# Cross attention key stacks filled from SBUF in narrow transfers, and projections split out of PSUM

## The chip, the cores and the metric

The kernel runs on one core of one Trainium2 chip. The metric is the time of the device for the whole program, in microseconds (us); the time before is the median of three runs. The chip has TensorE (PE in the profile; its weight loads are PEld), VectorE (DVE), ScalarE (ACT), GpSimd (POOL) and SyncE (SP), which here only issues transfers.

## What is computed

Four layers run over 32 sequences of 100 tokens with 128 features (`T` = 3,200 tokens, a chunk is four sequences, 400 tokens). Layers 0, 1 and 3 are transformer layers, layer 2 is a router layer that the change doesn't touch. A transformer layer has self attention, cross attention to a context of 1,444 tokens a sequence, and an MLP. The cross attention of layer 0 is this (16 heads of 8 features):

```
q_c = _ln(x) @ W_qc + b_qc
kv_c = _ln(context) @ W_kvc + b_kvc
k_c, v_c = split(kv_c, 2)
w = softmax(einsum('bhqd,bhsd->bhqs', q_c, k_c) * scale)
x = x + (einsum('bhqs,bhsd->bhqd', w, v_c) merged) @ W_cproj + b_cproj
```

Layer 1 takes the context without a norm, and layer 3 takes it turned, as layer 1 has kept it in memory.

## The kernel before

The phases follow one another, with a barrier between two. Every product of queries and keys is made from three bfloat16 parts of each float32 number (high, middle, low), whose six products of parts stand below one another as rows of a *stack*: the contraction over the stack's rows gives the score in nearly full precision.

**Projections** (`project_phase`, line 379). TensorE projects eight chunks into the eight banks of PSUM. VectorE copies a chunk with bias and scale to the float32 buffer `sq` (line 438). ScalarE makes the high part (170), GpSimd subtracts it from `sq` (180), ScalarE makes the middle part (173), GpSimd the low one (184); each step runs over all eight chunks before the next begins. With two projections (queries and keys of self attention) the second read of a chunk waits for the first low part of it, as `sq` is shared. SP stores a chunk when its low part is there (191; for the cross attention queries, 200, two transfers a chunk).

**Cross attention** (`cross_attention_phase`, 951) takes one sequence, or batch, a time, in a pipeline of slots written out by hand: in the slot of batch b TensorE makes the scores and values of b, the maximum tiles of b + 1 (from tile 16) and, from the last third of the slot, those of b + 2; it turns and projects the context of b + 3, and SP loads that of b + 5. Three buffers (`LAG`) exist of the stacks, values and contexts, but one of the parts `kparts` and one of the float32 keys `kf`. The work of a slot on each queue:

- TensorE: twelve blocks of context tokens; in each two groups of scores (1124), four maximum tiles (1103), the values (1141) and some of the preparation (1072, 1080, 1086). The scores of a batch wait for its negated maxima in the query stack.
- VectorE: 48 row maxima from PSUM (1260), then the row maximum, its negation and its three parts (1266 to 1284).
- ScalarE: the exponentials (1215) and copies of the preparation (1181, 1187, 1193).
- GpSimd: `pool_split_keys` (1328), the four steps that make the parts of the keys of b + 3, in one piece (layer 0) or three. It waits until the parts of the batch before have been written to memory. In layer 0 it also norms the context.
- SP (`sp_slot`, 1415), in this order: `sp_stacks` (1365) of b + 2, the load of the context, `sp_out` (1402) of b - 1, which stores the sums, waits for them, and brings them back rearranged, the store of the turned context (layer 1), `sp_negmax` (1380) of b + 1, and `sp_keys_out` (1394) of b + 3.

The key stack has 2 x 64 rows for eight pairs of heads. Before, `sp_keys_out` writes the parts in six transfers into a stack in memory (`ctx_k_stack`), whose rows of ones have been written there once, in layer 0, from a buffer that VectorE clears (1482) and SP stores (1517). `sp_stacks` waits for the scores of the batch that used the buffer and for the writes, and loads the whole stack in one transfer of all 128 partitions (1371); then it loads the queries in twelve transfers of eight partitions (1378). Self attention (line 801) loads its query stacks in twelve transfers of eight partitions from memory, and its key stacks (804) in six of 16 partitions.

## Time and profile before

| | |
|---|---|
| median of three runs | 5857.7 us (5855.48 to 5859.36) |
| the profiled execution, its own time | 5862.12 us |
| its span, first to last instruction | 5859.9 us |
| busy share of the span | PE 85%, DVE 66%, ACT 50%, POOL 26% |
| moved by transfers | 764.81 MB in 481,590 packets |
| mean granted TensorE clock | 0.897 |

The span is the time from the first to the last instruction of the profiled execution; the 2.2 us around it are the start and end of the program. The busy share is an average over phases with different limits, so the change is to be read from the phases it touches: the three cross attention phases, and the projection phases ahead of self and cross attention. A granted clock of 1.00 is 2.4 GHz, 0.50 is 1.2 GHz. In the rows of a stretch the numbers stand in the order PE, PEld, DVE, ACT, POOL (busy us and instructions), granted clock, share of the 16 DMA engines, GB/s. In rows in order of time, "idle before" is the time that the engine stood still ahead of the row, with what released it.

### The profile page before, as it was taken

How to read it: one execution, taken by the hardware profiler on the slowest of the kernel's cores; microseconds unless marked ns; L12 is line 12 of the kernel's file. 1: busy time of each engine (PE TensorE's matmuls, PEld its weight loads, DVE VectorE, ACT ScalarE, POOL GpSimd, SP SyncE). 2: the span in 40 equal slices, each digit the busy share in tenths (PEclk: the TensorE clock that was granted, in tenths of full speed). 3: DMA queues.
4: the chain of work that ended last, by engine and by line, in shares of the span. 5: the costliest groups of instructions: out<-in, count | busy, mean ns of one | idle time of the engine just before them, and what ended most of it. 6: DMA issues, size and time to landing. Idle time of an engine off the chain costs nothing. (4 is left out here: it accounts for less than half of the span.)

```text
span 5859.9 us, 149756 instructions
## 1 busy us (share of the span) xinstructions
PE 4994.4 (85%) x63358; PEld 3189.8 (54%) x63358; DVE 3843.7 (66%) x7732; ACT 2905.6 (50%) x4287; POOL 1546.6 (26%) x1270
## 2 busy tenths in 40 slices
PE   4848999999997577999999987899586899999998
PEld 2624555555563443666666653565363466666664
DVE  4537788788864445777777762544353688888883
ACT  2324666666664232666666654213223356666655
POOL 2034344344310213332333310000302333333320
PEclk6667999999997666999999998999766799999998
DMA  3334554554520525566555520530241555555540
GB/s 80 64 87 149 163 162 150 171 155 153 170 84 10 91 54 173 186 192 193 172 187 185 190 89 25 190 124 0 54 74 45 172 178 177 180 178 175 178 144 16
DMA packets 481590, 764.81 MB, mean 131 GB/s; under 512 B 144922, under 2 KB 381882, under 8 KB 468538
## 3 DMA queue, kind: packets, MB, share of 16 engines
q1 hardware_dynamic: 472090, 744.18, 42.8%
q10 hardware_dynamic: 8832, 11.07, 0.9%
q8 instruction: 500, 8.19, 0.6%
q14 instruction: 168, 1.38, 0.1%
HBM read 465.48 MB, written 287.75 MB: 129 GB/s over the span
## 5 line engine op out<-in xcount | busy, mean ns | idle before, releaser
L1260 DVE TENSOR_REDUCE maxima<-ps 100x1 f32<-100x482 f32 (+1 forms) x4608 | 2719.9, 649 | 834.3 <-PE ps L1103 827.6
L1215 ACT ACTIVATE probs<-ps 128x800 f32<-128x800 f32 (+1 forms) x2304 | 1799.4, 835 | 606.9 <-PE ps L1124 605.0
L1103 PE MATMUL ps<-kst,qst 48*100 48x482 bf16 (+1 forms) x4608 | 1102.7, 412 | 100.7 <-DMA qst<-cross_q_parts 49.5
L1312 POOL TENSOR_TENSOR kparts<-kf,zero 128x512 bf16<-128x512 f32 (+2 forms) x448 | 545.9, 1219 | 2109.1 <-ACT kf L1187 2069.8
L1141 PE MATMUL ps<-probs,vals 128*9 128x100 f32 x36864 | 1012.8, 250 | 5.5 <-ACT probs L1215 0.8
L1124 PE MATMUL ps<-qst,kst 128*128 128x200 bf16 (+1 forms) x9216 | 999.6, 251 | 11.9 <-DMA qst<-nparts 5.8
L1124 PEld LDWEIGHTS ps<-qst,kst 128*128 128x128 bf16 (+1 forms) x9216 | 761.7, 98 | 266.0 <-issue 152.5
L1141 PEld LDWEIGHTS ps<-probs,vals 128*9 128x9 f32 x36864 | 734.5, 90 | 255.4 <-issue 225.5
L1103 PEld LDWEIGHTS ps<-kst,qst 48*100 48x100 bf16 x4608 | 335.7, 120 | 617.9 <-DVE maxima L1260 326.6
L1193 ACT ACTIVATE vals<-ps 128x512 f32<-128x512 f32 (+1 forms) x288 | 161.9, 562 | 494.0 <-PE ps L1086 494.0
L1187 ACT ACTIVATE kf<-ps,perm_b_L 128x512 f32<-128x512 f32 (+1 forms) x288 | 190.4, 661 | 356.8 <-PE ps L1080 346.1
L1080 PE MATMUL ps<-ctxT,perm_wk_L 128*128 128x512 f32 (+1 forms) x576 | 306.6, 635 | 64.6 <-DVE maxima L1260 32.5
L729 ACT ACTIVATE probs<-ps 100x800 f32<-100x800 f32 x192 | 159.7, 837 | 365.3 <-PE ps L677 364.2
L1343 POOL TENSOR_TENSOR kparts<-kf,kparts 128x512 bf16<-128x512 f32 (+2 forms) x224 | 306.2, 1367 | 17.6
L1339 POOL TENSOR_TENSOR kf<-kf,kparts 128x512 f32<-128x512 f32 (+2 forms) x224 | 305.0, 1362 | 17.6
L741 DVE TENSOR_REDUCE maxima<-ps 100x4 f32<-100x400 f32 x384 | 205.2, 570 | 141.0 <-PE ps L655 140.4
L655 PE MATMUL ps<-kst 96*100 96x100 bf16 x1152 | 142.1, 285 | 146.6 <-DMA kst<-k_parts 118.1
L1086 PE MATMUL ps<-wkv_L,ctxT 128*128 128x128 f32 (+1 forms) x1536 | 227.9, 293 | 36.6 <-DVE maxima L1260 33.5
L1086 PEld LDWEIGHTS ps<-wkv_L,ctxT 128*128 128x128 f32 (+1 forms) x1536 | 184.3, 190 | 91.7 <-DVE maxima L1260 79.1
L655 PEld LDWEIGHTS ps<-kst 96*100 96x100 bf16 x1152 | 117.4, 190 | 172.0 <-issue 119.9
L180 POOL TENSOR_TENSOR sq<-sq,parts 128x400 f32<-128x400 f32 x72 | 65.7, 944 | 540.1 <-ACT parts L170 540.0
L1072 PE MATMUL ps<-ident,ctok 128*128 128x128 f32 (+1 forms) x768 | 131.6, 292 | 89.6 <-POOL ctok L1325 47.3
(253 smaller groups left out, 4634.4 us busy)
## 6 DMA issues: line engine op xcount, KB each, us to landing
kst<-ctx_k_stack SPq DMA_DIRECT2D x96, 2888.0 KB
ctx_k_stack<-kparts SPq DMA_DIRECT2D x192, 541.5 KB
ctx_k_stack<-kparts SPq DMA_DIRECT2D x192, 361.0 KB
ctok<-in_ctx_dram SPq DMA_DIRECT2D x64, 704.0 KB
ctx_k_stack<-kparts SPq DMA_DIRECT2D x192, 180.5 KB
ctx_turned<-ctxT SPq DMA_DIRECT2D x32, 722.0 KB, 3.4
cT<-ctx_turned SPq DMA_DIRECT2D x32, 722.0 KB, 5.7
ctxT<-ctx_turned SPq DMA_DIRECT2D x32, 722.0 KB
```

What stands on the lines that cost most here:

```text
L655: ins = nc.tensor.matmul(ps[0:N, o:o + N], queries[s][0:SROWS, h // 2, q0:q0 + N], keys[0:SROWS, h // 2, k0:k0 + N], start=True, stop=True)
L741: nc.vector.tensor_reduce(maxima[:, t // 4, c:c + 4], ps[0:N, at:at + CH].rearrange("p (h k) -> p h k", h=4), AX.X, ALU.max).then_inc(m_re ...
L1080: ins = nc.tensor.matmul(ps[:, at:at + w], wk, turned[s][:, a:a + w], start=True, stop=True)
L1086: ins = nc.tensor.matmul(ps[0:n, at + 128 * q:at + 128 * q + 128], turned[s][:, 128 * kt:128 * kt + n], wv, start=True, stop=True)
L1103: nc.tensor.matmul(ps[0:N, at:at + w], g.qst[s][row0:row0 + CROWS, j, N * e:N * e + N], g.kst[s][row0:row0 + CROWS, j, a:a + w], start=Tru ...
L1124: ins = nc.tensor.matmul(ps[0:kts[kt], o:o + 2 * N], g.kst[s][0:KROWS, 4 * hf + jj, 128 * kt:128 * kt + kts[kt]], g.qst[s][0:KROWS, 4 * hf ...
L1141: ins = nc.tensor.matmul(ps[q:q + VW, o:o + N], vals[s][:, kt, h, :], probs[kt % 2][hf][:, N * (2 * jj + e):N * (2 * jj + e) + N], start=( ...
L1215: nc.scalar.activation(probs[kt % 2][hf][0:kts[kt], :].rearrange("p (k n) -> p k n", k=2), src, ACT.Exp).then_inc(exp_done, 1)
L1260: nc.vector.reduce_max(maxima[:, col:col + 1], ps[0:N, at:at + widths[c]], AX.X).then_inc(m_read, 1)
L1312: return nc.gpsimd.tensor_tensor(out, src, g.zero[0:src.shape[0], 0:1].to_broadcast(list(src.shape)), ALU.add)
L1339: nc.gpsimd.tensor_tensor(kf[:, a:z], kf[:, a:z], parts[:, 0, a:z], ALU.subtract).then_inc(split, 1)
L1343: nc.gpsimd.tensor_tensor(parts[:, 2, a:z], kf[:, a:z], parts[:, 1, a:z], ALU.subtract).then_inc(parts_ready, 1)
```

## The change

*Cross attention.* There is no stack in memory any more. `sp_stacks` waits for the scores as before and for the parts of the keys, then issues twelve transfers, six rows of the stack for each of the two halves; each goes from 64 partitions of `kparts` to eight partitions of the stack, 64 rows of 2,888 bytes (1,444 bfloat16 numbers). The twelve query loads follow. `sp_keys_out` is gone. GpSimd now waits for these twelve transfers of the batch before (`k_loaded`) before it splits the next keys, and TensorE's first maximum tile waits for all twelve. The rows of ones stand in the three stacks in SBUF: in every layer VectorE clears all three stacks at the start of the phase, and SP waits for that ahead of its first slot. The six stores of ones are gone.

*Projections.* The four steps of a split are interleaved by chunk. Chunks that are `banked` keep their float32 value in the PSUM bank, and VectorE makes their two subtractions there; the others go through `sq` and GpSimd as before. With one projection (the queries of cross attention) the even chunks are banked; with two, all chunks of the second, and none of the first. The second projection no longer waits for the first to leave `sq`. The stores wait for the count of the engine that made the low part.

```diff
-def act_split(g, act, f, parts, f_ready, high, rest, middle):
-
-    for c in chunks(act):
-        act.wait_ge(f_ready, c + 1)
-        g.nc.scalar.activation(parts[:, 0, bass.ds(c * CH, CH)], tok(f, c), ACT.Copy).then_inc(high, 1)
-    for c in chunks(act):
-        act.wait_ge(rest, c + 1)
-        g.nc.scalar.activation(parts[:, 1, bass.ds(c * CH, CH)], tok(f, c), ACT.Copy).then_inc(middle, 1)
-
-
-def pool_split(g, pool, f, parts, high, rest, middle, low):
-
-    for c in chunks(pool):
-        pool.wait_ge(high, c + 1)
-        g.nc.gpsimd.tensor_tensor(tok(f, c), tok(f, c), parts[:, 0, bass.ds(c * CH, CH)],
-                                  ALU.subtract).then_inc(rest, 1)
-    for c in chunks(pool):
-        pool.wait_ge(middle, c + 1)
-        g.nc.gpsimd.tensor_tensor(parts[:, 2, bass.ds(c * CH, CH)], tok(f, c),
-                                  parts[:, 1, bass.ds(c * CH, CH)], ALU.subtract).then_inc(low, 1)
...
+class Split:
+
+
+
+    def __init__(self, sem, i, banked, parts, f):
+        self.banked, self.parts, self.f = banked, parts, f
+        self.f_ready, self.high, self.middle = sem(f"proj_read{i}"), sem(f"high{i}"), sem(f"middle{i}")
+        self.dve_rest, self.pool_rest = sem(f"dve_rest{i}"), sem(f"pool_rest{i}")
+        self.dve_low, self.pool_low = sem(f"dve_low{i}"), sem(f"pool_low{i}")
+
+    def part(self, k, c):
+        return self.parts[:, k, CH * c:CH * c + CH]
+
+    def value(self, g, c):
+        return bank(g, c) if c in self.banked else tok(self.f, c)
+
+    def nth(self, c):
+        return len([x for x in range(c + 1) if (x in self.banked) == (c in self.banked)])
+
+    def rest(self, c):
+        return self.dve_rest if c in self.banked else self.pool_rest
+
+    def low(self, c):
+        return self.dve_low if c in self.banked else self.pool_low
+def dve_split(g, dve, s, full, bias, scale):
+    for c in range(NCH + 2):
+        if c < NCH:
+            dve.wait_ge(full, c + 1)
+            g.nc.vector.tensor_scalar(s.value(g, c), bank(g, c), bias, scale, ALU.add, ALU.mult).then_inc(s.f_ready, 1)
+        if 0 <= c - 1 < NCH and c - 1 in s.banked:
+            dve.wait_ge(s.high, c)
+            g.nc.vector.tensor_tensor(bank(g, c - 1), bank(g, c - 1), s.part(0, c - 1), ALU.subtract).then_inc(s.dve_rest, 1)
+        if 0 <= c - 2 < NCH and c - 2 in s.banked:
+            dve.wait_ge(s.middle, c - 1)
+            g.nc.vector.tensor_tensor(s.part(2, c - 2), bank(g, c - 2), s.part(1, c - 2), ALU.subtract).then_inc(s.dve_low, 1)
+
+
+def act_split(g, act, s):
+    for c in range(NCH + 1):
+        if c < NCH:
+            act.wait_ge(s.f_ready, c + 1)
+            g.nc.scalar.activation(s.part(0, c), s.value(g, c), ACT.Copy).then_inc(s.high, 1)
+        if c:
+            act.wait_ge(s.rest(c - 1), s.nth(c - 1))
+            g.nc.scalar.activation(s.part(1, c - 1), s.value(g, c - 1), ACT.Copy).then_inc(s.middle, 1)
+
+
+def pool_split(g, pool, s):
+    copied = [c for c in range(NCH) if c not in s.banked]
+    for c, before in zip(copied + [None], [None] + copied):
+        if c is not None:
+            pool.wait_ge(s.high, c + 1)
+            g.nc.gpsimd.tensor_tensor(tok(s.f, c), tok(s.f, c), s.part(0, c), ALU.subtract).then_inc(s.pool_rest, 1)
+        if before is not None:
+            pool.wait_ge(s.middle, before + 1)
+            g.nc.gpsimd.tensor_tensor(s.part(2, before), tok(s.f, before), s.part(1, before), ALU.subtract).then_inc(s.pool_low, 1)
...
-        f_ready = [sem(f"proj_read{i}") for i in range(npart)]
-        high = [sem(f"high{i}") for i in range(npart)]
-        rest = [sem(f"rest{i}") for i in range(npart)]
-        middle = [sem(f"middle{i}") for i in range(npart)]
-        low = [sem(f"low{i}") for i in range(npart)]
+        banked = [(), tuple(range(NCH))] if npart == 2 else [tuple(range(0, NCH, 2))]
+        splits = [Split(sem, i, banked[i], parts[i], sq) for i in range(npart)]
...
-                    for c in chunks(dve):
-                        dve.wait_ge(full[i], c + 1)
-                        if i:
-                            dve.wait_ge(low[i - 1], c + 1)
-
-                        nc.vector.tensor_scalar(tok(sq, c), bank(g, c), bias, scale, ALU.add,
-                                                ALU.mult).then_inc(f_ready[i], 1)
+                    dve_split(g, dve, splits[i], full[i], bias, scale)
...
-    K_RUNS = ((0, 3), (3, 2), (5, 1))
-    KW = 16 * 2 * len(K_RUNS)
+    KL = 16 * 2 * len(SLOT_K)
...
-                wait(g.pe, k_loaded[s], 16 * (r + 1))
+                wait(g.pe, k_loaded[s], KL * (r + 1))
...
-            wait(pool, k_written[p.s], KW * (p.r + 1))
+            wait(pool, k_loaded[p.s], KL * (p.r + 1))
...
             wait(sp, st_full, H2 * (b - LAG + 1))
-            wait(sp, k_written[s], KW * (r + 1))
-            sp.dma_start(g.kst[s][:, :, :].rearrange("p j n -> p (j n)"), g.kscr[s]).then_inc(k_loaded[s], 16)
+            wait(sp, parts_ready, len(CUTS) * (b + 1))
+            for slot, part in enumerate(SLOT_K):
+                for e in range(2):
+                    at = HALF * e + HD * slot
+                    src = parts[HALF * e:HALF * e + HALF, part, :]
+                    sp.dma_start(g.kst[s][at:at + HD, :, :], src).then_inc(k_loaded[s], 16)
...
-        def sp_keys_out(k):
-            b, s, r = k.b, k.s, k.r
-            sp = g.sp
-            wait(sp, parts_ready, len(CUTS) * (b + 1))
-            for first, n in K_RUNS:
-                for e in range(2):
-                    sp.dma_start(slot_rows(s, e, first, n), parts[HALF * e:HALF * e + HALF, 0:n, :]).then_inc(k_written[s], 16)
...
-            if slot.k(3) is not None:
-                sp_keys_out(slot.k(3))
...
-                if normed:
-                    nc.vector.memset(g.kst[0][:, :, :].rearrange("p j n -> p (j n)").bitcast(F32), ONE_PAIR).then_inc(stacks_set, 1)
+                for s in range(LAG):
+                    nc.vector.memset(g.kst[s][:, :, :].rearrange("p j n -> p (j n)").bitcast(F32), ONE_PAIR).then_inc(stacks_set, 1)
...
-                if normed:
-                    sp.wait_ge(stacks_set, 1)
-                    for s in range(LAG):
-                        for e in range(2):
-                            rows = slice(HALF * e + CROWS, HALF * e + HALF)
-                            sp.dma_start(g.kscr[s][rows, :], g.kst[0][rows, :, :].rearrange("p j n -> p (j n)")).then_inc(ones_written, 16)
-                    sp.wait_ge(ones_written, 16 * 2 * LAG)
+                sp.wait_ge(stacks_set, LAG)
```

## Rows read from the trace of the kernel before

**Rows 1.** Busy time by engine in a stretch of each cross attention phase; then clock, DMA share, GB/s
```profile
600.00:1600.00 1000.00, 923.45 (x14169) 594.18 (x14167) 811.17 (x1987) 659.52 (x916) 422.14 (x200) 1.00 0.51 158
2400.00:3400.00 1000.00, 949.31 (x14837) 621.94 (x14836) 768.73 (x1404) 616.39 (x882) 322.57 (x312) 1.00 0.58 185
4700.00:5600.00 900.00, 850.68 (x13907) 557.33 (x13909) 735.78 (x1343) 545.19 (x771) 312.49 (x300) 1.00 0.57 177
```

**Rows 2.** Waits in 2400 to 3400 us: us in total, times, longest
```profile
PEld ps L1124 <- DMA qst<-nparts: 2.2, 4, 1.5
```

**Rows 3.** Order in time of SP's queue, one batch of layer 1: start, us, issue
```profile
2795.63 4.13 SPq L1387 DMA_DIRECT2D qst<-nparts  x6
2799.81 8.54 SPq L1400 DMA_DIRECT2D ctx_k_stack<-kparts  x6
...
2811.55 0.33 SPq L1371 DMA_DIRECT2D kst<-ctx_k_stack  x1
2811.92 8.35 SPq L1378 DMA_DIRECT2D qst<-cross_q_parts  x12
...
2826.51 2.56 SPq L1411 DMA_DIRECT2D oT<-o_sums  x4
...
2834.04 4.13 SPq L1387 DMA_DIRECT2D qst<-nparts  x6
```

**Rows 4.** Order in time of TensorE, last scores and first new maximum tile
```profile
2798.84 0.86 PE L1124 MATMUL ps<-qst,kst 128*36 128x200 bf16 x8
...
2829.76 0.42 PE L1103 MATMUL ps<-kst,qst 48*100 48x482 bf16 x2
```

**Rows 5.** Order in time of VectorE, row maxima of two batches, layers 0 and 3
```profile
1053.49 0.20 DVE L1266 TENSOR_REDUCE rowmax<-maxima 100x16 f32<-100x48 f32 x1
...
1093.84 0.20 DVE L1266 TENSOR_REDUCE rowmax<-maxima 100x16 f32<-100x48 f32 x1
...
5109.82 0.20 DVE L1266 TENSOR_REDUCE rowmax<-maxima 100x16 f32<-100x48 f32 x1
...
5146.00 0.20 DVE L1266 TENSOR_REDUCE rowmax<-maxima 100x16 f32<-100x48 f32 x1
```

**Rows 6.** Stretches with one kind of transfer each; last two columns: DMA share, GB/s
```profile
100.00:102.50 2.50, 0.00 (x0) 0.00 (x0) 0.00 (x0) 0.00 (x0) 0.09 (x1) 0.50 1.11 318
2801.10:2803.90 2.80, 2.64 (x46) 1.63 (x45) 2.33 (x5) 1.57 (x2) 0.00 (x0) 1.00 0.98 198
2804.00:2810.00 6.00, 5.76 (x76) 4.26 (x78) 4.02 (x8) 3.12 (x5) 0.00 (x0) 1.00 0.93 273
1949.00:1951.50 2.50, 0.00 (x0) 0.00 (x0) 0.00 (x0) 0.00 (x0) 0.00 (x0) 0.50 0.58 50
1950.50:1954.00 3.50, 0.00 (x0) 0.00 (x0) 0.00 (x0) 0.00 (x0) 0.00 (x0) 0.50 0.58 75
1960.00:1967.50 7.50, 6.08 (x44) 4.94 (x43) 5.77 (x12) 0.00 (x0) 0.00 (x0) 0.50 0.59 76
2244.00:2246.50 2.50, 0.00 (x0) 0.00 (x0) 0.00 (x0) 0.00 (x0) 2.41 (x3) 0.50 0.64 141
```

**Rows 7.** Order in time at the start of layer 1's phase: GpSimd, SP, TensorE
```profile
2211.41 1.04 POOL L1312 TENSOR_TENSOR kparts<-kf,zero 128x512 bf16<-128x512 f32 x1 [7.05 <-ACT kf L1187]
...
2224.57 8.57 SPq L1400 DMA_DIRECT2D ctx_k_stack<-kparts  x6
...
2247.04 1.01 PE L1103 MATMUL ps<-kst,qst 48*100 48x482 bf16 x3 [20.51 <-DMA qst<-cross_q_parts]
```

**Rows 8.** Order in time of VectorE, layer 0: the memset of a key stack
```profile
397.66 4.87 DVE L1482 MEMSET kst<- 128x5776 f32 x1 [1.15 <-issue]
```

**Rows 9.** VectorE's read of PSUM (line 438); order in time of GpSimd and SP
```profile
L438 DVE TENSOR_SCALAR sq<-ps,perm_b_L x24: 632/634/636, 363.5 to 4501.9; 128x400 f32<-128x400 f32 x24
...
373.70 10.57 SPq L200 DMA_DIRECT2D cross_q_parts<-parts  x16
...
85.67 7.23 POOL L180 TENSOR_TENSOR sq<-sq,parts 128x400 f32<-128x400 f32 x8
```

More of the change, by code:

```diff
@@ L188, in sp_parts_out @@
-def sp_parts_out(g, sp, parts, dram, low, stored):
+class Split:
[14 more added lines that the diff above has]
+        return self.dve_low if c in self.banked else self.pool_low
@@ L189, in sp_parts_out, with sp_queries_out @@
+def sp_parts_out(g, sp, parts, dram, split, stored):
     for c in chunks(sp):
-        sp.wait_ge(low, c + 1)
+        sp.wait_ge(split.low(c), split.nth(c))
         sp.dma_start(dram[:, :, bass.ds(c * CH, CH)], parts[:, :, bass.ds(c * CH, CH)]).then_inc(stored, 16)
     sp.wait_ge(stored, 16 * NCH)
-def sp_queries_out(g, sp, parts, low, stored):
+def sp_queries_out(g, sp, parts, split, stored):
     for c in range(NCH):
-        sp.wait_ge(low, c + 1)
+        sp.wait_ge(split.low(c), split.nth(c))
@@ L418, in _ @@
                     pe_linear(g, pe, [w], [lambda c: tok(xin, c)], xin_ready, xin_per, free, full[i])
-                    free = f_ready[i]
+                    free = splits[i].f_ready
             @block.vector
@@ L450, in _ @@
                 for i in range(npart):
-                    act_split(g, act, sq, parts[i], f_ready[i], high[i], rest[i], middle[i])
+                    act_split(g, act, splits[i])
             @block.gpsimd
@@ L455, in _ @@
                 for i in range(npart):
-                    pool_split(g, pool, sq, parts[i], high[i], rest[i], middle[i], low[i])
+                    pool_split(g, pool, splits[i])
             @block.sync
@@ L461, in _ @@
                     if dram is g.qx:
-                        sp_queries_out(g, sp, parts[i], low[i], stored[i])
+                        sp_queries_out(g, sp, parts[i], splits[i], stored[i])
                     else:
-                        sp_parts_out(g, sp, parts[i], dram, low[i], stored[i])
+                        sp_parts_out(g, sp, parts[i], dram, splits[i], stored[i])
 class attention_close_sems:
@@ L1013, in cross_attention_phase @@
         split, parts_ready = sem("split_steps"), sem("parts_ready")
-        k_written, k_loaded = slots("k_written"), slots("k_loaded")
+        k_loaded = slots("k_loaded")
         qst_loaded, neg_loaded = slots("qstack_loaded"), slots("negmax_loaded")
@@ L1020, in cross_attention_phase @@
         ones, zeros, ctx_std, stacks_set = sem("ones"), sem("zeros"), sem("ctx_std"), sem("stacks_set")
-        ones_written, queries_zeroed, ctx_kept = sem("ones_written"), sem("queries_zeroed"), sem("ctx_kept")
+        queries_zeroed, ctx_kept = sem("queries_zeroed"), sem("ctx_kept")
         set_up = 1 + 2 * LAG
-        def slot_rows(s, e, first, n):
-            return g.kscr[s].rearrange("(e r d) (j n) -> e (d j) r n", e=2, d=HD, j=PAIRS)[e, :, first:first + n]
         def max_tile(slot, x):
@@ L2039, in program @@
     g.ctxT = nc.dram_tensor("ctx_turned", (B, P, S), F32).ap()
-    g.kscr = [nc.dram_tensor(f"ctx_k_stack{s}", (P, PAIRS * S), BF16).ap() for s in range(LAG)]
     g.oself = [nc.dram_tensor(f"o_self_sums{s}", (P, CH), F32).ap() for s in range(LAG)]
```

## The prediction, made before the change was run

> **What bounds the kernel now.** I read the stretches first. In the three cross attention phases, which fill about 3,900 of the 5,860 us, TensorE is busy 92 to 95 per cent of the time at the full granted clock (1.00, the 2.4 GHz level), VectorE 77 to 82, and the transfers take a share of 0.51 to 0.58 of the 16 DMA engines [rows 1]. The reader is to see that TensorE has little idle time left for anyone to give back. The waits of 1,000 us of layer 1 say the same from the other side: the only transfer that TensorE waits for is that of the negated maxima, 2.2 us in four waits of weight loads [rows 2]; the key stacks are never waited for there. So in the steady part the trip through memory costs nothing, and the change can gain only at the edges; it can lose wherever the new transfers are later than the old ones.
>
> The queue of SyncE (SP) shows how much later they may be. One batch of layer 1 takes 38.41 us, from the maxima issue at 2795.63 to the next at 2834.04. In it SP spends 8.54 us on six writes of parts to memory, waits until 2811.55 for them to land, spends 0.33 us on the wide load and 8.35 us on twelve query loads; after the sums of the batch before are out it waits again, until 2826.51 [rows 3]. TensorE ends the last scores of a batch at about 2799.7 and first uses the next batch's stack at 2829.8, 30 us later [rows 4]. The other two layers run at 40.35 us and 36.18 us a batch [rows 5].
>
> **The change, part by part.**
>
> *Removed:* per batch six writes (8.54 us of SP, 2.22 MB), the wait behind them, and one load of 2.96 MB. None is on the path in the steady part.
>
> *Added:* twelve transfers of 64 rows of 2,888 bytes, 2.22 MB in all, each from 64 partitions into eight. They can be issued as soon as SP has sent the maxima and the old stack is free, near 2799.8 in the batch shown, 11.75 us ahead of today's load. Issue costs SP about 0.70 us each by the query loads of the same shape (8.35 over twelve) [rows 3], 8.4 us together. What decides is D, the time in which the data moves. The trace of before has no such transfer, so I bound it from both sides.
>
> - Upper speed: a store over all partitions moves 318 GB/s on 16 engines [rows 6]. Loads into eight partitions keep the share at 0.58, that is, they use eight engines [rows 6]. Half of 318 is 159 GB/s, and D = 2.218 MB / 159 = 14 us.
> - Lower speed: while only one half of the parts is read (64 partitions) all 16 engines are busy at 0.98 and yet move 198 GB/s; once both halves are in flight it is 273 [rows 6]. Something that belongs to the partitions saturates. By plain proportion eight would get 24.8 GB/s, which the next rows exclude; the slowest stretch in which transfers into few partitions ran in a backlog is 50 GB/s [rows 6], D = 44.4 us.
> - The nearest row: self attention loads its query stacks with transfers of just this form, 64 rows, eight engines, eight partitions of destination, and in a backlog they run at 75 and 76 GB/s, twice over [rows 6]. Its rows are shorter (800 bytes) and come from memory. I take 76: D = 29.2 us. That it is above 50 I read as neighbouring transfers overlapping on different partitions.
>
> The Trainium skill says, in SBUF — State Buffer, section "Door 1: The DMA port swizzle (why [64,N] ≈ [32,N])", that DMA bandwidth follows the number of SBUF ports that the partitions reach, and gives 196 GB/s for 64 partitions and 104 for 16. The 198 of the trace agrees with it; by that rule eight partitions would get about half of 104, an estimate of 52 GB/s and a D near 43 us. It speaks against this change, where the 76 of the trace is milder.
>
> *What D does.* Two loops close over one batch. (A) The parts have one buffer: GpSimd may not split the next keys before the last narrow transfer has landed, where it now waits only for the writes. From the first issue: 1.3 us to the first data, D, 1.5 us to landing (both as in rows 3 and 6: issue 2799.81, data from 2801.1, data until 2810, next step 2811.55), then the split, 13.1 us from 2211.41 to 2224.5 [rows 7], and 0.2 us of signals: D + 16.1. (B) SP is in order. The sums stand in the same DMA rings behind the keys, 2.5 us of queries [rows 6], about 2.3 us of the next context and 0.5 of their own, and SP waits for them; then come 3.6 us of small issues and 4.2 us for the maxima [rows 3], and only then the next keys: 1.3 + D + 2.5 + 2.3 + 0.5 + 1.5 + 3.6 + 4.2 = D + 15.9; without the context store of layer 1, D + 15.5 in layer 0. Behind SP's wait stand the maxima, and behind those TensorE's scores.
>
> With D = 29.2: layer 0, 44.7 against 40.35, +4.35; layer 1, 45.3 against 38.41, +6.9; layer 3, 45.3 against 36.18, +9.1. Together 20.3 us for each batch; 29 of the 31 intervals count, since two in the filling are longer already: +590 us.
>
> *Filling.* At the start of each phase the maxima wait for stack and queries: now 22.5 us from the last split (2224.57 to 2247.04) [rows 7]. After: 1.3 + D + 2.5 + 1.5 = 34.5 us, +12 in each of three phases: +36.
>
> *Clearing.* Three memsets of a stack (4.87 us each, 14.6) [rows 8] stand in place of one and six stores. VectorE has nothing to do before 2247, and the parts that SP waits for come at 2224.5, past 2202 + 14.6 = 2217 [rows 7]. I cost them at nothing; uncovered they would be 10 to 15 us a phase.
>
> *Projections.* The query projection of cross attention is paced by its stores: GpSimd's first low part is ready at 373.7, 10.2 us after the first read of PSUM at 363.5, and SP then needs 10.57 us for sixteen issues [rows 9]. With even chunks split by VectorE out of PSUM and steps interleaved, the first low part comes after about 4 us (0.63 per read, some 0.55 for each following step); the stores end at 14.6 at the earliest, and near 16 because odd chunks still take two GpSimd steps of 0.90 us: 4 to 6 us gained, 4.7 taken, times three is 14. The double projections are now one unbroken GpSimd row, 32 steps of 0.90 us (eight in 7.23) [rows 9]. After, GpSimd does the queries (14.5 us) and ScalarE, which is in order, starts on the keys only then; VectorE needs 8 x (0.63 + 0.57 + 0.57) = 14.2 us for them. 28.7 against 29: I take 1.3 us each, 4 together. Sum -18.
>
> **Sum.** +590 + 36 - 18 = +608 us on the profiled execution, whose span is 5859.9 and whose own time is 5862.1, 4.4 above the median of 5857.7. On the median that is 6465 us.
>
> **Rivals.**
>
> *The narrow transfers are quick enough; faster.* For it: the 76 may come from reading short rows of memory, which is not done here, and eight engines at their full pace give 159. The Trainium skill adds, in DMA: Bandwidth & Descriptors, section "Why small descriptors are slow (HBM only)", that SBUF to SBUF transfers don't suffer from small pieces; no run here shows it yet. Against it: the 198 of the trace, which is a read of SBUF itself with the same long rows. Its price: with D = 14 nothing closes, the filling is bound by issue (8.4 + 8.35 + 3.0 = 19.7 against 22.5, -2.8 three times), so 5857.7 - 18 - 8 = 5831 us. It decides where 3(D - 17.2) + 29(D - 20.1) = 18, at D = 20.4 us, that is 109 GB/s. Chance 0.36, and 0.06 for a rate so near this point that nothing can be told.
>
> *No overlap at all; much slower.* Twelve transfers at 50 GB/s, D = 44.4: 29 x (19.5 + 22.1 + 24.3) + 82 - 18 = +1,975, 7,833 us. For it: these transfers are 3.6 times as long as the ones that gave 76, so neighbours overlap less; this is also where the port rule leads. Chance 0.14.
>
> *The projections don't gain:* stores stay the pace, and 18 shrinks to 8. The quick case would then be 5841 us, still faster.
>
> **How the numbers follow.** The forecast, 60 to 109 GB/s around 76, has 0.44, its own range being 5,880 to 7,200. Slower in all: 0.58, faster 0.36, same 0.06; 0.2 per cent (12 us) is about what a measurement of this kernel can tell from no change. The range goes from 5,825, a little below the quick case, to 7,300, which is D near 38.5 us, 58 GB/s; it leaves out most of the case without overlap. TensorE's granted clock is 0.50 (1.2 GHz) in stretches where it had stood idle [rows 6]; waits long enough to bring that back would add to the slow cases, and I leave them at the upper end.
>
> **What would show it.** A share near 0.5 and about 76 GB/s at the start of every batch; GpSimd's first key step waiting for the keys' transfer and not for ScalarE; SP waiting longer for the sums; TensorE waiting for the stacks or the maxima; batches of about 45 us in all three layers. If instead the batches stay at 40.35, 38.41 and 36.18, D is under 20 us and I am wrong in its term alone. If they grow and GpSimd doesn't wait for transfers, it is loop B and not A.

## The result, and the profile after the change

The changed kernel takes 7207.4 us, median of four runs (7189.1 to 7219.1); the kernel before, timed beside it, 5856.6 us. The ratio is 1.230, 95% interval 1.228 to 1.232: 1,350.8 us slower. The forecast was 6465 us, slower too, but by 608 us.

The stretches of the three cross attention phases come first, as in [rows 1] (TensorE, its weight loads, VectorE, ScalarE and GpSimd busy, then the granted clock, the DMA share and GB/s):

```profile
600.00:1600.00 1000.00, 772.67 (x10903) 489.76 (x10901) 632.10 (x1528) 509.01 (x707) 319.72 (x152) 0.87 0.50 66
2800.00:3800.00 1000.00, 755.81 (x10868) 487.30 (x10871) 569.72 (x1029) 453.09 (x648) 238.99 (x232) 0.85 0.54 80
5600.00:6500.00 900.00, 655.11 (x9559) 418.06 (x9560) 512.75 (x923) 375.45 (x531) 214.47 (x208) 0.83 0.48 66
```

TensorE was busy 92 to 95 per cent at the full clock; now it is 73 to 77 per cent at a mean of 0.83 to 0.87. The DMA share has hardly moved, but the bytes behind it fell from 158 to 185 GB/s to 66 to 80: the same occupation of the engines carries less than half. The waits of the whole execution (microseconds, times, longest) name who stands still:

```profile
POOL kparts L1335 <- DMA kst<-kparts: 3369.2, 93, 41.9
...
PE ps L1126 <- issue: 836.9, 90, 14.7
...
PE ps L1126 <- DMA qst<-cross_q_parts: 137.2, 6, 31.9
```

GpSimd waits for the new transfers before each split, 93 times for 96 batches. TensorE waits 96 times at line 1126, the maximum tiles, 974 us in all. Ninety of these are put down to "issue", that is, to nothing the profile shows; what they really are comes out below. SP's queue in one batch of layer 1, against [rows 3] (start, duration, issue):

```profile
3071.83 9.06 SPq L1398 DMA_DIRECT2D kst<-kparts  x12
3080.94 22.48 SPq L1405 DMA_DIRECT2D qst<-cross_q_parts  x12
3103.47 2.58 SPq L1385 DMA_DIRECT2D ctok<-in_ctx_dram  x1
...
3112.30 0.36 SPq L1426 DMA_DIRECT2D o_sums<-osb  x1
3117.28 2.60 SPq L1430 DMA_DIRECT2D oT<-o_sums  x4
...
3120.97 4.48 SPq L1414 DMA_DIRECT2D qst<-nparts  x6
3125.97 9.04 SPq L1398 DMA_DIRECT2D kst<-kparts  x12
```

and GpSimd and TensorE in the same batch, each line ending with the idle time before it and what ended it:

```profile
3111.91 1.04 POOL L1335 TENSOR_TENSOR kparts<-kf,zero 128x512 bf16<-128x512 f32 x1 [40.46 <-DMA kst<-kparts]
```

```profile
3115.11 0.64 PE L1126 MATMUL ps<-kst,qst 48*100 48x482 bf16 x2 [13.17 <-issue]
```

The keys are first issued at 3071.83 and have landed at 3111.9, 40 us later; the query loads, issued behind them, took 8.35 us of SP before and now 22.48, because the issue itself is held up; TensorE gets its first new maximum tile at 3115.11, 3.2 us after the keys, where the old kernel had it 30 us after the start of the batch [rows 4]; the next keys go out at 3125.97. That batch is 54.1 us long. The stretches inside such a transfer give its rate (last three columns: clock, DMA share, GB/s):

```profile
3133.00:3136.00 3.00, 2.83 (x27) 2.61 (x26) 1.27 (x3) 1.31 (x3) 0.00 (x0) 1.00 0.53 61
3136.00:3139.00 3.00, 2.84 (x46) 1.86 (x45) 2.37 (x4) 1.45 (x3) 0.00 (x0) 1.00 0.52 60
...
3169.00:3172.00 3.00, 2.16 (x13) 1.32 (x11) 2.18 (x6) 1.03 (x2) 2.76 (x4) 0.50 0.06 13
```

The last of them lies behind TensorE's wait in the next batch: the granted clock is at 0.50, the 1.2 GHz level. The first two show the rate, 60 to 61 GB/s at a share of 0.52: 2.218 MB take 36 us, not 29. From the first to the last row maxima of a phase (31 intervals) a batch takes 52.07, 52.23 and 52.55 us in the three layers; before it took 39.99, 38.28 and 36.18. Single batches lie between 39 and 64 us. The means add up to 31 x (12.08 + 13.95 + 16.37) = 1,314 us of the 1,351. At the start of layer 0's phase the way from the first key issue to the first maximum tile is 43.2 us, where from the issue of the writes behind the last split it was 22.75:

```profile
415.49 8.95 SPq L1398 DMA_DIRECT2D kst<-kparts  x12
```

```profile
458.67 1.01 PE L1126 MATMUL ps<-kst,qst 48*100 48x482 bf16 x3 [30.58 <-DMA qst<-cross_q_parts]
```

### The profile page after: what moved, and what is told of

The parts are those of the page before. It is cut to its first block and busy times, and to the rows that moved or that the text cites. A ratio compares the mean times of both kernels' runs of the same rounds, so it can differ in the third digit from the quotient of the medians.

```text
span 7187.2 us, 150216 instructions
## 1 busy us (share of the span) xinstructions
PE 5298.2 (74%) x63358; PEld 3347.7 (47%) x63358; DVE 3950.7 (55%) x7812; ACT 2906.8 (40%) x4287; POOL 1477.3 (21%) x1198
## 5 line engine op out<-in xcount | busy, mean ns | idle before, releaser
L1126 PE MATMUL ps<-kst,qst 48*100 48x482 bf16 (+1 forms) x4608 | 1154.1, 447 | 1023.8 <-issue 836.9
L1164 PE MATMUL ps<-probs,vals 128*9 128x100 f32 x36864 | 1136.2, 268 | 96.6 <-issue 89.1
L1147 PE MATMUL ps<-qst,kst 128*128 128x200 bf16 (+1 forms) x9216 | 1101.7, 266 | 29.8 <-issue 18.5
L1164 PEld LDWEIGHTS ps<-probs,vals 128*9 128x9 f32 x36864 | 813.7, 96 | 402.4 <-issue 310.9
L1147 PEld LDWEIGHTS ps<-qst,kst 128*128 128x128 bf16 (+1 forms) x9216 | 829.5, 104 | 324.7 <-issue 220.7
L1103 PE MATMUL ps<-ctxT,perm_wk_L 128*128 128x512 f32 (+1 forms) x576 | 325.9, 670 | 57.9 <-DVE maxima L1283 30.0
L1103 PEld LDWEIGHTS ps<-ctxT,perm_wk_L 128*128 128x128 f32 x576 | 100.0, 206 | 164.5 <-DVE maxima L1283 102.9
```

The source lines that it names most:

```text
L1103: ins = nc.tensor.matmul(ps[:, at:at + w], wk, turned[s][:, a:a + w], start=True, stop=True)
L1126: nc.tensor.matmul(ps[0:N, at:at + w], g.qst[s][row0:row0 + CROWS, j, N * e:N * e + N], g.kst[s][row0:row0 + CROWS, j, a:a + w], start=Tru ...
L1147: ins = nc.tensor.matmul(ps[0:kts[kt], o:o + 2 * N], g.kst[s][0:KROWS, 4 * hf + jj, 128 * kt:128 * kt + kts[kt]], g.qst[s][0:KROWS, 4 * hf ...
L1164: ins = nc.tensor.matmul(ps[q:q + VW, o:o + N], vals[s][:, kt, h, :], probs[kt % 2][hf][:, N * (2 * jj + e):N * (2 * jj + e) + N], start=( ...
```

## The experiments

### Which part of the change costs and which gains

**Projections alone** (cross attention as before; the classes and loops of the projections as changed).

```
 cross_attention_phase: as before, with ctx_k_stack in memory
 project_phase: Split, dve_split, act_split, pool_split as in the change
```

> The projections of the change alone, cross attention as before. My terms of the prediction: 14 us for the three query projections and 4 us for the double ones, so 5839 us (-18). Rival: the stores of the parts are the pace and stay it, -8 us, 5849 us. If the batches of cross attention still take 40.35, 38.41 and 36.19 us, the projections have no part in the 1,350 us.

Measured: 5823.8 us against 5854.8, ratio 0.9947 (0.9934 to 0.9960): -31 us, batches unchanged. The gain is real and larger than worked out. SP's stores show where, against [rows 9]:

```profile
73.67 12.22 SPq L229 DMA_DIRECT2D q_parts<-parts  x8
88.08 8.26 SPq L229 DMA_DIRECT2D k_parts<-parts  x8
...
99.73 4.15 SPq L830 DMA_DIRECT2D kst<-q_parts  x12
...
366.60 12.24 SPq L238 DMA_DIRECT2D cross_q_parts<-parts  x16
```

The query projection's stores now end at 378.84, 16.1 us after the first read of PSUM at 362.79; before it was 384.27 - 363.49 = 20.8. The difference is the 4.7 us of the prediction to the tenth. The double projection, for which I had taken 1.3 us, gave more: the first stack load of self attention starts at 99.73 and started at 104.25, 4.5 us. Both were read in layer 0 alone; three times their sum is 27.6 of the 31 us.

**Keys alone** (projections as before).

```
 project_phase, act_split, pool_split: as before
 cross_attention_phase: as in the change
```

> The key stacks alone by narrow transfers (with the three memsets), projections as before. Theory: all of the loss is here, so the time of the whole change plus what the projections gain: 7207 + 18 = 7225 us. With the rival on the projections (-8) it is 7215 us. Batches of 52.1 to 52.5 us in all three layers, as in the whole change.

Measured: 7239.2 us, ratio 1.2367 (1.2348 to 1.2386), +1,384 us; batches 51.93, 52.62 and 52.56 us. The two parts add up: 1,384 - 31 = 1,353 against 1,351. Of the 1,384 the batches are 31 x (11.94 + 14.34 + 16.38) = 1,322, and the 62 left are some 21 us for each of the three fillings: from the last split to the first maximum tile it is 43.2, 44.1 and 44.1 us here, and 22.8, 22.5 and 22.6 in the kernel before. The memsets have no part in that: in the changed kernel the first keys of all three phases go out 0.03 us after the last step of the split, and the memsets have ended 7.0, 3.8 and 0.7 us before.

### What sets the rate of the transfers

**Half of the keys** (the upper 64 partitions left out).

```
-                for e in range(2):
+                for e in range(1):
```

> The transfers into the upper 64 partitions are left out, six of twelve with half of the bytes; the rest of the computation runs on what the memset left there. Theory that a rate holds (36 us for 2.2 MB, 62 GB/s): 18 us for 1.1 MB, below the 20 us at which the loops close, so the batches are back at 40.35, 38.41 and 36.2 us and the time is near 5835 us. Rival, that the time of a batch goes by something else than the length of the transfers (TensorE's stalls, the clock at 0.81): batches stay above 45 us and the time above 6400 us. If two transfers on opposite halves were really working side by side, half of them would take nearly as long as all: batches of 45 us or more too, but with the share of the DMA engines at half of what it is now.

Measured: 5933.4 us, one run; batches 40.78, 39.26 and 37.67 us. Most of them are back at the old length to the hundredth, with some of 42 to 46 us between them (the last section has what is known of them). The six transfers of the lower half run at the rate that the twelve of both had, and take half the time, 18.1 us on average from the first packet to the last against 35.8:

```profile
2822.00:2825.00 3.00, 2.92 (x50) 1.76 (x46) 3.00 (x6) 1.76 (x3) 0.00 (x0) 1.00 0.55 66
2825.00:2828.00 3.00, 2.83 (x25) 2.49 (x24) 1.43 (x3) 1.16 (x3) 0.00 (x0) 1.00 0.54 62
```

So it is a rate, and transfers into opposite halves of SBUF do not run side by side on SP's queue.

**The same bytes into 48 partitions** (16 transfers; the stacks then hold keys in another arrangement).

```
-            for slot, part in enumerate(SLOT_K):
+            for slot in range(PAIRS):
                 for e in range(2):
-                    at = HALF * e + HD * slot
-                    src = parts[HALF * e:HALF * e + HALF, part, :]
-                    sp.dma_start(g.kst[s][at:at + HD, :, :], src)...
+                    src = parts[HALF * e:HALF * e + CROWS, SLOT_K[slot % 6], :]
+                    sp.dma_start(g.kst[s][HALF * e:HALF * e + CROWS, slot, :], src)...
```

> The same bytes (2.2 MB a batch) from the same parts, but as sixteen transfers of 48 rows into 48 partitions, where it was twelve of 64 rows into 8; the stacks then hold other numbers, so the result is another. Theory that the eight partitions of the destination set the rate: it goes up to between 198 GB/s (the trace's read of 64 partitions) and 273, D is 8 to 11 us plus issue of 16 x 0.7, and the batches are back at 40.35, 38.41 and 36.2 us: 5835 us. Rival, that transfers inside SBUF are slow whatever their shape (rows of 2,888 bytes, 64 descriptors each): D stays at 30 us or more and the time above 6,900 us.

Measured: 5808.8 us, batches 40.35, 38.41 and 36.19 us. The transfers run at

```profile
2811.00:2814.00 3.00, 2.76 (x45) 1.64 (x45) 3.00 (x7) 1.57 (x2) 0.00 (x0) 1.00 0.89 227
2814.00:2817.00 3.00, 3.00 (x31) 2.61 (x35) 0.98 (x2) 1.61 (x3) 0.00 (x0) 1.00 0.79 201
```

A transfer inside SBUF with rows of 2,888 bytes is not slow as such. This run alone leaves open whether more partitions or more engines (a share of 0.79 to 0.89, not 0.52) make it fast; the runs with other row orders decide that.

**From memory instead of SBUF** (two transfers put the parts in memory; the same twelve load the stacks from there).

```
-                    src = parts[HALF * e:HALF * e + HALF, part, :]
+                    src = g.kscr[s][HALF * e:HALF * e + HALF, part, :]
```

> The parts go to memory first (two transfers), and the same twelve narrow transfers of 64 rows of 2,888 bytes then load the stacks from there. Theory that the destination's eight partitions are the bound: the rate stays at 60 to 66 GB/s though the source is memory, GpSimd waits no longer for the stacks (its loop is gone), but the queue's loop (D + 15.5) still makes batches of 51 to 52 us: 7100 to 7250 us. Rival, that the source in SBUF was slow: D falls to 14 to 20 us and the time to 5830 to 5900 us.

Measured: 7396.4 us, one run; batches 53.82, 54.97 and 53.90 us. The rate is

```profile
3105.00:3108.00 3.00, 2.84 (x33) 2.06 (x22) 1.84 (x4) 1.45 (x4) 0.00 (x0) 1.00 0.50 63
3108.00:3111.00 3.00, 2.84 (x47) 1.68 (x44) 2.33 (x4) 2.07 (x4) 0.00 (x0) 1.00 0.53 66
```

at the same share as from SBUF. The source plays little part: on average the keys take 32.4 us from the first packet to the last, against 35.8. (The batches are 2 us longer still, since SP also waits for the writes.)

**Eight partitions, but six apart** (and the query stacks to match).

```
-                    at = HALF * e + HD * slot
+                    at = HALF * e + slot
-                    sp.dma_start(g.kst[s][at:at + HD, :, :], src)...
+                    sp.dma_start(g.kst[s][at:at + 43:6, :, :], src)...
```

> The rows of the stacks in another order: row 6d + slot where it was 8 slot + d, so that each of the twelve transfers writes eight partitions that lie six apart and not side by side (the query stacks, which must match, too). The same count of transfers, rows and bytes. Theory that neighbouring partitions share a way in and that this set the 62 GB/s: the rate goes up to at least 109 GB/s and, with eight engines at their pace in the trace, to 159; D is 14 to 20 us, the batches are back at 40.35, 38.41 and 36.19 us and the time is 5800 to 5830 us. The Trainium skill, SBUF - State Buffer, section Door 1, gives 8 adjacent partitions two ports (an estimate of 52 to 54 GB/s) and these eight rows seven of them. Rival, that eight partitions or eight engines are slow wherever they lie: nothing changes, 7207 us and batches of 52 us.

Measured: 5820.0 us against 5856.4, ratio 0.9943 (0.9930 to 0.9957); batches 40.35, 38.41 and 36.18 us.

```profile
2817.00:2820.00 3.00, 2.92 (x46) 1.69 (x46) 3.00 (x6) 1.69 (x3) 0.00 (x0) 1.00 0.51 164
2820.00:2823.00 3.00, 2.83 (x27) 2.56 (x26) 1.34 (x3) 1.25 (x3) 0.00 (x0) 1.00 0.52 155
```

The same twelve transfers, rows and bytes, the same eight engines (share 0.51), and 2.6 times the rate. The 159 GB/s that the prediction worked out as the pace of eight engines is met.

**Two apart.**

```
-                    at = HALF * e + HD * slot
+                    at = HALF * e + 16 * (slot // 2) + slot % 2
-                    sp.dma_start(g.kst[s][at:at + HD, :, :], src)...
+                    sp.dma_start(g.kst[s][at:at + 15:2, :, :], src)...
```

> Between the change (the eight partitions of a transfer side by side) and the spread order (six apart): now two apart, over 16 partitions. Theory that groups of neighbouring partitions share a way in, so that the rate goes by how many groups are reached: twice as many as side by side, 62 x 2 = 124 GB/s, D near 18 us, just under the 20 us where the loops close: batches at 40.35, 38.41 and 36.19 us with some longer ones, 5820 to 5930 us. Rival, that it is the eight partitions together with something that only the wide spacing avoids: 62 GB/s and 7200 us.

Measured: 5834.4 us, ratio 0.9966 (0.9954 to 0.9978).

```profile
2823.00:2826.00 3.00, 2.92 (x69) 1.86 (x57) 3.00 (x6) 2.15 (x3) 0.00 (x0) 1.00 0.51 117
2826.00:2829.00 3.00, 2.84 (x23) 2.38 (x23) 1.80 (x4) 0.79 (x2) 0.00 (x0) 1.00 0.52 117
```

Twice the span of partitions, twice the rate (60 to 117), at the same share of the engines and still with eight partitions a transfer. With the six-apart order at 155 to 164, still at that share, the rate rises with how far the written partitions spread; 48 partitions at 201 to 227 use more engines. By the Trainium skill, SBUF — State Buffer, section "Door 1: The DMA port swizzle (why [64,N] ≈ [32,N])", groups of four neighbours share a port: eight side by side reach two of 16, two apart four, 48 partitions eight, an estimate of 54, 109 and 218 GB/s. The traces agree, with 60, 117 and 201 to 227; the first two lie 7 to 11 per cent above the estimates. Six apart, the eight rows reach six or seven ports by that mapping, an estimate of 163 to 190 GB/s, so there the pace of eight engines, 159, comes first.

### Which loop turns 36 us of transfer into 52 us of batch

**GpSimd's loop (A) opened:** the parts are freed one by one.

```
-            wait(pool, k_loaded[p.s], KL * (p.r + 1))      (ahead of the whole split)
+            wait(pool, k_in[0][p.s], ...)  ahead of the copies of part 0
+            wait(pool, k_in[1][p.s], ...)  ahead of part 1
+            wait(pool, k_in[2][p.s], ...)  ahead of part 2
```

> GpSimd waits for the parts one by one: the transfers go in the order of the parts, the first part may be overwritten after six of twelve, and only the last three steps of the split wait for the last transfer. Loop A shrinks from D + 16.1 to about D + 6.2 us; loop B (SP's queue in order, D + 15.5 to 15.9) is as it was. Theory that both loops were closed at almost the same length: batches of 51 to 52 us still, 7150 to 7207 us. Rival, that GpSimd's loop alone was the bound: batches of 43 to 47 us and a time of 6200 to 6800 us.

Measured: 7196.9 us, ratio 1.2290 (1.2273 to 1.2306); batches 51.99, 52.41 and 52.22 us. The numbers are those of the theory of two equal loops, but a third loop gives them too, as the next runs show.

**SP's loop (B) opened:** the loads behind the sums go after the next keys.

```
             if slot.k(2) is not None:
                 sp_stacks(slot.k(2))
+            if slot.k(-2) is not None:
+                sp_out_rest(slot.k(-2))     (was the second half of sp_out(slot.k(-1)))
```

> Only SP's loop opened, with the slow transfers (adjacent rows, SP's queue) as in the change: the four loads and one that follow the sums of a batch are issued after the next batch's keys and queries, so that SP no longer waits for a transfer that stands behind the keys. Theory that GpSimd's loop closes by itself at D + 16.1, some 51 to 52 us: the batches stay, 7100 to 7210 us. Rival, that GpSimd's wait only mirrors SP's: batches of 47.8 us or less (SP's own occupation: 9.0 keys, 22.0 queries, 8.7 context, 0.4, 3.1, 0.4 and 4.5), 6720 us or less.

Measured: 7103.0 us, one run; batches 50.64, 51.33 and 51.44 us. **Both opened,** with the two edits together:

> Both loops opened with D as it is (the parts freed one by one, and the loads behind the sums issued after the next keys). Theory that two loops of almost the same length set the batch: only now does it get shorter, down to the next limit; SP's own occupation with rings that are full, 47.8 us, gives 5824 + 856 + 36 = 6716 us; if its issues are held up less, the chain over three stacks (43.3, 41.3 and 39.1 us) gives 6133. I expect the first. Rival, that something else holds 52 us: 7200 us.

Measured: 7088.0 us, one run; batches 50.95, 51.28 and 51.09 us. Neither of my two limits came; the rival without a name did. With both loops open something else still holds 51 us, and the waits of this kernel name it, this time with its releaser:

```profile
PE ps L1128 <- DMA qst<-cross_q_parts: 892.3, 89, 38.9
```

That is a third loop, C. A slot begins when TensorE has ended the last scores of a batch and so freed its stack. Keys and queries for that stack are issued there, and TensorE, in order, comes to their first maximum tile 30 us later in the same slot. If they are not there it stops, and the next slot can't begin before it has gone on. In the changed kernel itself all 22 batches between 2800 and 4000 us show it: from the first key issue to the first maximum tile 41.74 us, from there to the next key issue 10.92, together 52.67. The two stretches of the kernel before are 30.0 and 8.4 us (2799.8, 2829.8, 2838.2, by [rows 3, 4] and the batch of 38.41).

What SP waits for last, ahead of each key issue, shows which loop closes. The last scores on the stack that the issue at 3125.97 fills:

```profile
3125.08 0.86 PE L1147 MATMUL ps<-qst,kst 128*36 128x200 bf16 x8
```

They end at 3125.94, 0.03 us before the issue. From the fifth batch of each phase on, the freed stack is the last of the three conditions in 74 of the 84 batches of the changed kernel; the parts have then been ready for 1.3 us on average and SP free for 1.2 us. With the parts freed one by one it is 78 of 84, and the parts are ready 10.3 us ahead. So loops A and B end just short of C, and C holds the batch.

**The queries taken from behind the keys** (both loops open, query loads on GpSimd's queue).

```
+        def pool_queries(k):
+            wait(pool, st_full, H2 * (b - LAG + 1))
-                        sp.dma_start(g.qst[s][at:at + HD, ...], src)...
+                        pool.dma_start(g.qst[s][at:at + HD, ...], src)...
```

> Both earlier loops opened, and besides the twelve query loads go through GpSimd's queue, so that they no longer stand behind the keys. Theory of a third loop, seen in the run before: TensorE's first maximum tile of a batch waits in order for the keys and the queries that were first issued at the start of the same slot (42 us after the first key issue, where it used to be needed at 30), and the next stack is only free at the end of that slot, 8.4 to 11.5 us later. Without the queries behind the keys the wait ends at 1.3 + D + 1.5 = 38.8 us instead of 42.1, so each of 93 batches is 3.3 us shorter: 7088 - 307 = 6780 us, and TensorE waits at that tile for the keys. Rival, that TensorE's wait isn't what closes the loop: 7050 to 7100 us still.

Measured: 6954.1 us, one run; batches 49.23, 50.12 and 49.70 us: 134 us less, not 307. In one batch of layer 1 SP and TensorE show

```profile
3110.04 10.17 SPq L1422 DMA_DIRECT2D kst<-kparts  x12
...
3160.43 9.58 SPq L1422 DMA_DIRECT2D kst<-kparts  x12
```

```profile
3149.07 0.64 PE L1128 MATMUL ps<-kst,qst 48*100 48x482 bf16 x2 [8.93 <-issue]
```

39.0 us to the first tile, as worked out, and 11.4 to the next keys. Between 2800 and 4000 us the means are 39.66 and 10.74 us (23 batches), where with both loops open they were 40.73 and 10.52 (22): the batch follows TensorE's wait, but the wait shrank by 1.1 us and not by 3.3. From the last key packet to the first tile it is 1.2 us on average where it was 3.9, but the key packets themselves now take 37.0 us where it was 35.6; that they share the way with the queries would explain this. The direction bears loop C out, and so does the last condition of the key issue, the freed stack in 73 of 84 batches here and in 74 with both loops open.

**Keys on GpSimd's queue,** with the parts freed one by one, and without:

```
-                    sp.dma_start(g.kst[s][at:at + HD, :, :], src)...
+                    pool.dma_start(g.kst[s][at:at + HD, :, :], src)...   (after waits for st_full and parts_ready on POOL)
```

> As the kernel that frees the parts one by one, and the twelve key transfers are issued by GpSimd on its own queue, so that the sums and maxima don't stand behind them in SP's: both loops open, D unchanged at some 36 us. What is left is the chain over three stacks: (D + 2.8 + three batches - 30)/3, that is 43.3, 41.3 and 39.1 us a batch, +2.9 over before 31 times in three layers: 5824 + 273 + 36 for the filling = 6133 us, and up to 200 more for TensorE's gaps. Rival, that the bytes themselves or another wait behind them hold the batch at 50 us and more: over 7000 us.

> Only the second loop opened: GpSimd issues the key transfers on its own queue, adjacent rows as in the change, but still splits the next keys only after the last transfer has landed. Theory of two loops: GpSimd's (D + 16.1) stays closed, batches of 51 to 53 us, 7150 to 7250 us. Rival, that SP's order was the real bound and GpSimd's loop only touches it: batches below 47 us, under 6800 us.

Measured: 6443.0 and 6398.6 us, one run each; batches 45.30, 44.26, 43.21 and 43.95, 44.08, 43.35 us. Both expectations took D as unchanged, and it was not: it is some 23 us here. So the first fell with its rival, and the second run, whose numbers are those of its rival (batches below 47 us, under 6800), doesn't show that SP's order was the bound. The last section shows what changed in the transfers. The stack waits are nearly gone, and what keeps these kernels 4 to 7 us a batch above the old ones was not taken further; the breaks described there are 237 us of it in the second.

**Queries ahead of the keys,** on the six-apart order:

```
             wait(sp, st_full, H2 * (b - LAG + 1))
+            (twelve query loads)
             wait(sp, parts_ready, len(CUTS) * (b + 1))
             (twelve key transfers)
-            (twelve query loads)
```

> The spread order, and the twelve query loads issued ahead of the keys. In the steady part nothing waits for either, so the batches stay as they are; in the filling of each phase the queries go out before the first parts are ready, and their 8.3 us of issue and 2.5 us of transfer leave the way to the first maxima: 3 x 8 to 11 us, 5790 us against 5820. Rival, that the first keys have to wait behind the queries in the rings for as long: 5820 us.

Measured: 5849.3 us against 5855.7, ratio 0.9989 (0.9980 to 0.9998), some 29 us above the plain six-apart order and not 30 below. At the start of layer 1's phase the six-apart kernel has SP idle only from 2201.8 to 2204.4, when the parts are ready: no room for 9.1 us of query issue. Here the queries go out from 2204.7, the keys only from 2213.8, and the first maximum tile comes at 2231.6 instead of 2224.7. In the steady part the keys come close to loop C's 30 us, and what SP does behind them is late as well: in layer 3 TensorE waits for keys three times, 2.8 us in all, and for the negated maxima 11 times, 10.3 us (twice, 1.5 us, in the six-apart kernel). Batches of 38 to 41 us appear there, and the layer's mean goes from 36.17 to 36.91.

## Why the prediction was right and where it failed

*What bounds, and that the trip through memory cost nothing:* right. With the transfers fast, the batches are at 40.35, 38.41 and 36.18 us, just as with the old route.

*D, 29.2 us at 76 GB/s:* this is **the step that failed**. It is 36.4 us by loop C (41.7 - 1.3 - 2.5 - 1.5), 61 GB/s by the stretches, and 35.8 us on average between the first and the last key packet of a batch, 62 GB/s. I took the nearest row by the shape of the transfers, and read the extra over 50 as neighbours overlapping. Neighbours on opposite halves don't overlap here, as the half kernel shows. Of the reservation in my own text (shorter rows, from memory) the second half is answered: from memory, with the long rows, it is 63 to 66 GB/s. The stretch at 75 holds loads into 16 partitions too, but the one at 76 does not owe its rate to them: between 1960.8 and 1965.3 us of the kernel before only query loads into eight partitions land, one of 51.2 KB every 0.70 us, which is 73 GB/s. They differ from the new transfers in two ways: neighbours in time go to partitions 0 to 7 and 8 to 15 of one half and not to opposite halves, and the rows have 800 bytes and not 2,888. Which of the two makes the difference from 76 to 61 no run tried, so why the row misled stays open; that the new transfers run at 61 is measured. The estimate that stood beside it, D near 43 us, was off as far on the other side.

*The loops:* A and B are there and are as long as I said (in the batch shown the split ends 0.9 us ahead of the next key issue, the maxima 0.5 us ahead), but opening either or both gives at most 119 us, since the freed stack comes last in 74 of 84 batches. The loop that binds is C, which I had in hand as "30 us later" and used as slack instead of as a limit: 1.3 + D + 2.5 + 1.5 to the first tile and 8.4 behind it, D + 13.7, and 2.5 more in the second stretch, where TensorE runs on after its wait with the granted clock partly at 0.50 (0.66 on average, and 1.00 before). That is D + 16.2, by chance the length of loop A, so the forecast was not wrong through it.

*The sum:* 20.3 us a batch for the three layers should have been 42.4. With D = 36.4 its own formula gives 41.9, or 42.5 against the mean batches of before, from which the 42.4 is taken. Counting 29 intervals left out 80 us more: the last two of a phase, 35 and 33 us before, are stretched to the full length as well. *Filling:* +36 us expected, 62 measured with the keys alone (52 in the profiled execution of the changed kernel, where the third took 34.5 us), mostly D again.

*Projections:* -18 expected, -31 measured. The query term was exact (4.7 us), the double one mis-sized (1.3 us taken, 4.5 found), both by layer 0. *Memsets:* nothing, as forecast.

*The rivals:* the quick case (5831 us at D = 14) didn't come, but the six-apart order is that case, with 155 to 174 GB/s, batches unchanged and 5820 us. The break-even point of 109 GB/s lies between two measured rates: at 117 the kernel is 0.34 per cent faster than before, at 61 it is 23 per cent slower. *No overlap at all* at 50 GB/s and 7833 us had the mechanism that the half kernel shows, with a rate 11 GB/s too low; its chance of 0.14 was too small.

## What to carry to other kernels

Ask of a narrow transfer not only how many partitions it touches but how far they lie apart: with the row order of the stacks changed from 8 slot + d to 6d + slot, the change gains 0.57 per cent instead of losing 23; of the kernels that compute the same, it is the fastest measured, level with the projections alone (5820.0 and 5823.8 us). A transfer that was hidden in a route with 30 us of slack is free up to those 30 us and costs at least what lies beyond them, once for every batch (here the first tile came 11.7 us later and the batch was 14.3 us longer); so work out, for the engine that reads the data in order, when its buffer is freed and when it is first used, before looking at who else waits. And where several waits close at almost the same length, removing one shows little: the reading of all of them, which condition comes last before each issue, told more than three of the experiments.

## What the runs showed of the hardware that I had not expected

**On GpSimd's queue the same transfers keep twice as many engines busy.** The twelve key transfers issued there: in one batch they are issued from 3101.88 and have landed at 3129.06, 27.2 us instead of some 38 to 40, and the stretch between runs at a share of 1.02, not 0.52:

```profile
3116.00:3119.00 3.00, 2.84 (x48) 1.98 (x47) 2.37 (x4) 2.01 (x4) 0.00 (x0) 1.00 1.02 104
```

```profile
q0 software_dynamic: 92160, 213.30, 29.3%
q1 hardware_dynamic: 375130, 245.09, 19.1%
```

(In the second fence: the queue, packets, MB, share of the span.) 104 GB/s is close to twice 60, as if both halves were now written at once; that reading is argued, not tested. The packets differ too: a batch of keys is 384 packets of 5,776 bytes there, and 768 of 2,888 on SP's queue. The Trainium skill, DMA: Bandwidth & Descriptors, section "Why a DMA increments its semaphore by 16 and not by 1", lets the shape choose the number of engines, eight here; on SP's queue the share of 0.52 agrees. On GpSimd's queue, by the same section, a transfer of fewer than 16 engines starts at an engine that moves on from one transfer to the next, and some copies get all 16. The share of 1.02 fits either, two transfers of eight engines at a time or one of sixteen, and no run here tells them apart.

**TensorE breaks off in the middle of a group of matmuls while narrow transfers run.** There are 28 such breaks of 1 us and more at line 1164 in the changed kernel, 89 us in all, 16 with 46 us in the half kernel, 61 with 237 us with the keys on GpSimd's queue, and none in the kernel before or in the six-apart order. One in the half kernel, and the instruction queue's row in the stretch 2988 to 2992.5 us (packets, MB, share):

```profile
2987.43 0.36 PE L1164 MATMUL ps<-probs,vals 128*9 128x100 f32 x8
2992.46 1.19 PE L1164 MATMUL ps<-probs,vals 128*9 128x100 f32 x24 [4.67 <-issue]
```

```profile
q8 instruction: 1, 0.02, 2.7%
```

Eight matmuls of a group of 32 run, then none for 4.67 us, in which one packet of instructions is moved. This is not by chance: each of the breaks of 2 us and more, 22 in the changed kernel, 11 in the half kernel and 56 with the keys on GpSimd's queue, has a packet of this queue (16,384 bytes) under way in it, where stretches of the same length at other times have one in 36 to 44 per cent of the cases. So the long breaks go with the loading of instructions. That TensorE's next instructions stood in a DMA engine behind the long packets would explain them, and the longer batches of the half kernel too; no run here proves it.

**Slow transfers hold up the issue of those behind them.** Twelve query loads cost SP 8.35 us to issue in the kernel before [rows 3] and 22.48 us behind the slow keys: a slow transfer is paid for by the queue that issues the next one, before anyone waits for its data.
